# Sixteen weighted rows: one running sum, or four scalings in place and one reduction

## The reference, cut to what matters

```
scores, idx = top_k(sim, 16)              # per half key, 128 candidates
score = scores[0][..., :, None] + scores[1][..., None, :]
final_scores, pk_idx = top_k(score, 16)   # the 16 best pairs
kv_scores = softmax(final_scores)
k = einsum('bnhk,bnhkd->bnhd', kv_scores, keys_table[ind])
v = einsum('bnhk,bnhkd->bnhd', kv_scores, values_table[ind])
sim = einsum('bihd,bjhd->bhij', q, k)     # causal softmax, attention, projection
```

## Time and profile before

| what | value |
|---|---|
| profiled execution | 2909.09 us, span 2907.2 us |
| median of the runs | 2908.06 us |
| DVE busy | 2381.6 us, 82% of the span |
| POOL busy | 1961.6 us, 67% |
| PE busy | 1606.5 us, 55% |
| ACT busy | 762.2 us, 26% |
| DMA | mean 100 GB/s |

### The profile page before, as it was taken

One profiled execution on the slowest core, in us unless ns is written; L12 is line 12 of the kernel. 1 busy time (PEld: TensorE's weight loads), 2 busy tenths in 40 slices (PEclk: granted clock), 3 DMA queues, 4 the chain that ended last, 5 costly groups with the idle time before them and its releaser, 6 DMA issues. The chain is left out here.

```text
span 2907.2 us, 31873 instructions
## 1 busy us (share of the span) xinstructions
PE 1606.5 (55%) x7386; PEld 1234.3 (42%) x7386; DVE 2381.6 (82%) x8326; ACT 762.2 (26%) x1884; POOL 1961.6 (67%) x2064
## 2 busy tenths in 40 slices
PE   6847735565456445563555445554555445654555
PEld 6846624453334334442344334442344333432444
DVE  6678889999788888888888878888888878888873
ACT  5737611222122211221122112221122112221122
POOL 0001767777777777777777777777777777777774
PEclk8958856786578656785677656775678567765677
DMA  4200223333333333333333333333333333333332
GB/s 159 96 1 10 79 86 106 108 105 106 105 108 106 107 105 105 108 105 106 105 108 105 106 105 108 105 106 106 105 108 105 106 105 108 105 107 105 105 105 76
DMA packets 109528, 291.26 MB, mean 100 GB/s; under 512 B 34128, under 2 KB 41808, under 8 KB 107344
## 3 DMA queue, kind: packets, MB, share of 16 engines
q0 software_dynamic: 98304, 268.57, 32.6%
q1 hardware_dynamic: 10080, 20.97, 2.1%
q10 hardware_dynamic: 1008, 0.33, 0.0%
HBM read 288.69 MB, written 1.05 MB: 100 GB/s over the span
## 5 line engine op out<-in xcount | busy, mean ns | idle before, releaser
L282 POOL DMA_INDIRECT ring<-table,rows x2048 | 1954.1, 954 | 749.7 <-issue 587.3
L736 DVE SCALAR_TENSOR_TENSOR ps<-ring,wgt,ps 128x256 f32<-128x256 f32 x1792 | 865.5, 483 | 316.6 <-DMA ring<-table,rows 290.3
L1529 PE MATMUL ps<-ident,work 128*128 128x128 f32 x1088 | 261.3, 400 | 531.2 <-PEq L1522 531.2
L1529 PEld LDWEIGHTS ps<-ident,work 128*128 128x128 f32 x1088 | 202.0, 211 | 586.1 <-issue 586.1
L1543 PE MATMUL ps<-pts,work 128*128 128x128 f32 x2176 | 422.2, 360 | 35.4 <-PEq L1541 34.6
L1543 PEld LDWEIGHTS ps<-pts,work 128*128 128x128 f32 x2176 | 384.7, 267 | 84.1 <-issue 81.6
L1514 PE MATMUL ps<-work,qT 128*128 128x512 f32 (+3 forms) x576 | 312.3, 683 | 65.3 <-PEq L1511 65.3
L1249 ACT ACTIVATE pts<-ps 128x512 f32<-128x512 f32 (+2 forms) x320 | 168.8, 533 | 337.9 <-ACTq L1248 337.6
L1241 ACT ACTIVATE work<-ps,nmax 128x128 f32<-128x128 f32 (+15 forms) x128 | 149.4, 1167 | 327.5 <-ACTq L1239 327.5
L1506 PE MATMUL ps<-ident,work 128*128 128x128 f32 x128 | 46.8, 366 | 322.8 <-PEq L1504 322.7
L1514 PEld LDWEIGHTS ps<-work,qT 128*128 128x128 f32 x576 | 125.5, 239 | 196.9 <-issue 196.9
(11 more groups left out here) (234 smaller groups left out, 2688.5 us busy)
## 6 DMA issues: line engine op xcount, KB each, us to landing
ring<-table,rows POOLq DMA_INDIRECT x2048, 2.8
staged<-adj_in SPq DMA_DIRECT2D x16, 1024.0 KB, 4.9
xs<-x_in SPq DMA_DIRECT2D x4, 256.0 KB, 6.4
wpkq<-w_pkq SPq DMA_DIRECT2D x8, 128.0 KB, 2.6
out<-xs SPq DMA_DIRECT2D x1, 832.0 KB, 4.4
keyd<-pk_keys SPq DMA_DIRECT2D x16, 32.0 KB, 2.8
wo<-w_o SPq DMA_DIRECT2D x8, 64.0 KB
out<-xs SPq DMA_DIRECT2D x1, 192.0 KB, 2.1
```

Of the source, the lines that this page charges most:

```text
L282: nc.gpsimd.indirect_dma_start(ring[:, t % RING, k, :], None, table_d, bass.IndirectOffsetOnAxis(ap=rows[:, t % RING, k:k + 1], axis=0),). ...
L736: return v.scalar_tensor_tensor(out, row, w, acc_ps, ALU.mult, ALU.add)
L1529: ins = m.transpose(ps[:, 2 + (parity + b) % 2, j % 4 * P:(j % 4 + 1) * P], prob[:, t % 2, j * P:(j + 1) * P], ident[:, :])
```

## The change

The sixteen dependent multiply-adds go. In their place, `scale_rows(t, q)` multiplies the four rows of quarter q in the ring by their weights, in place, in one instruction of 4 x 256 elements whose second operand is the weights, each repeated 256 times. When all four quarters are scaled, `add_rows(t)` sums the sixteen rows with one `tensor_reduce` of 4096 elements to 256: it reads, for each of the 256 columns, the sixteen values that lie 256 elements (1 KB) apart. The weights `wgt` move from SBUF to 64 columns of PSUM bank 0, where the running sum no longer lives; `acc` in SBUF becomes `first_kv`. Where the multiply-adds with their `settle()` stood between two pieces of the search, a `settle()` or a `v.drain()` takes their place. Semaphores between engines are as they were: a slot is still freed, and `kv_full` still raised, when the whole sum of the tile is done.

```diff
-        wgt = sb("wgt", [P, 4, TOPK])
-        acc = sb("acc", [P, 2, 2 * D])
+        first_kv = sb("first_kv", [P, 2 * D])
-        acc_ps = ps[:, 0, 0:2 * D]
+        wgt = ps[:, 0, 3 * D + 64:3 * D + 64 + 4 * TOPK].rearrange("p (s k) -> p s k", s=4)
...
-            def sum_rows(t, k):
-                row, w = ring[:, t % RING, k, :], wgt[:, t % 4, k:k + 1]
-                if k == 0:
-                    return v.tensor_scalar(acc_ps, row, w, None, ALU.mult)
-                out = acc_ps if k < TOPK - 1 else kv[:, t, :] if t > 0 else acc[:, 0, :]
-                return v.scalar_tensor_tensor(out, row, w, acc_ps, ALU.mult, ALU.add)
+            def scale_rows(t, q):
+                some = ring[:, t % RING, q * QK:(q + 1) * QK, :]
+                w = wgt[:, t % 4, q * QK:(q + 1) * QK].unsqueeze(2).to_broadcast([P, QK, 2 * D])
+                v.tensor_tensor(some, some, w, ALU.mult).then_inc(dve_done, c.one())
+            def add_rows(t):
+                out = kv[:, t, :] if t > 0 else first_kv[:, :]
+                return v.tensor_reduce(out, ring[:, t % RING, :, :].rearrange("p k c -> p c k"), X, ALU.add)
...
                 landed(h, t, 0)
-                sum_even(t, 0)
+                scale_rows(t, 0)
                 if find:
                     find_replace(a)
                 if out:
                     add_out_1((t - 2) % T)
...
-                sum_odd(t, 1)
-                sum_even(t, 2)
+                landed(h, t, 1)
+                scale_rows(t, 1)
+                settle()
                 if out:
                     add_out_2((t - 2) % T)
                 if find:
                     find_second(a)
                 if prev and (t - 1) % T < 8:
                     score_max((t - 1) % T)
-                sum_odd(t, 3)
-                landed(h, t, 1)
-                sum_even(t, 4)
+                v.drain()
                 if find:
                     find_index(a)
                 if prev and (t - 1) % T >= 8 and not (last and t == T - 1):
                     score_max((t - 1) % T)
-                sum_odd(t, 5)
-                sum_even(t, 6)
+                if weigh:
+                    weigh_1((t + AHEAD - 1) % T)
+                landed(h, t, 2)
+                scale_rows(t, 2)
+                settle()
                 if find:
                     find_rows(a)
                 if weigh:
-                    weigh_1((t + AHEAD - 1) % T)
-                sum_odd(t, 7)
-                landed(h, t, 2)
-                sum_even(t, 8)
+                    weigh_2((t + AHEAD - 1) % T)
+                v.drain()
                 if find:
                     find_pairs(a)
-                if weigh:
-                    weigh_2((t + AHEAD - 1) % T)
-                sum_odd(t, 9)
-                sum_even(t, 10)
+                landed(h, t, 3)
+                scale_rows(t, 3)
+                settle()
                 if find:
                     find_best(a)
-                sum_odd(t, 11)
-                landed(h, t, 3)
-                sum_even(t, 12)
-                if find:
+                    v.drain()
                     find_best_replace(a)
-                sum_odd(t, 13)
-                sum_even(t, 14)
-                if find:
+                    v.drain()
                     find_best_second(a)
-                settle()
                 if t == 0:
-                    sum_rows(t, TOPK - 1).then_inc(dve_done, c.one())
+                    add_rows(t).then_inc(dve_done, c.one())
                     settle()
                 else:
-                    sum_rows(t, TOPK - 1).then_inc(kv_full, 1)
+                    add_rows(t).then_inc(kv_full, 1)
                     v.drain()
```

More of the change, by code:

```diff
@@ L759, in landed @@
                 dve.wait_ge(gathered[t % RING][q], h * (16 * QK * (T // RING)) + 16 * QK * (t // RING + 1))
-            def sum_even(t, k):
-                sum_rows(t, k).then_inc(dve_done, c.one())
-            def sum_odd(t, k):
-                settle()
-                sum_rows(t, k).then_inc(dve_done, c.one())
-                settle()
             def find_halves(t):
@@ L808, in step @@
                 if t == 1:
-                    v.tensor_copy(kv[:, 0, :], acc[:, 0, :]).then_inc(kv_full, 1)
-                sum_odd(t, 1)
-                sum_even(t, 2)
+                    v.tensor_copy(kv[:, 0, :], first_kv[:, :]).then_inc(kv_full, 1)
+                landed(h, t, 1)
+                scale_rows(t, 1)
+                settle()
                 if out:
```

## The result

The changed kernel takes 3299.22 us (median of 4 runs, 3296.64 to 3301.6) against 2906.16 us for the kernel before (four runs now, 2904.01 to 2908.72), a ratio of 1.1353 with a 95% interval of 1.1336 to 1.1371. I had forecast slower, but 2968 us with a range to 3010. The direction was right, the size was not: +393 us in place of +60.

The account below looks back on a forecast made before the run. POOL's gather issue was taken as the limit; DVE's step, 17.28 - 7.35 + 4.9 + 4.54 + 0.68 = 20.05 us, uses the whole slack, so DVE's chain from step 0 gives 2968 us, own range 2935 to 3000, widened to 2922 to 3010.

Parts of the forecast that it names:

- The limit before, and the slack: Kernel before: POOL's gather issue sets the period, 20.01 us a tile; DVE needs 17.28 us, leaving 2.73 us a step.
- the scalings: DVE's new multiplications of ring quarters by their weights: 1.22 us each, four a step, 4.9 us.
- The sums that go: DVE's removed first multiply, seven pairs of multiply-adds (6.34 us), and last one with its drain: 7.35 us a step.
- the drains: Four pauses a step between dependent search pieces on DVE, 0.17 us each: 0.68 us, bounds 0 to 1.0.
- the late start: DVE begins step 0 at 378.74 us and, its pace now equal to POOL's, never makes up that lateness.
- the loop's returns: The loop over heads goes back five times; DVE's waits there, formerly in the slack, add 17.5 us.
- the last four steps: End of kernel, no search: 11.7 us to step 124's `kv`, then 14.8, 15.0 and 18.6 to the next ones.
- the hand-over through PE: From `kv` to score maximum: 6.51 us for tile 14; rival: a wait every step, 3095 us, chance 0.03.
- The reduction: DVE's new 4096-element sum each step: 4.40 us without stride penalty, 4.54 us with its drain.
- the strided reduction is slower: Rival: two cycles an element in DVE's reduction, 4.3 us more a step, about 3515 us; chance 0.08.
- The rule that I had cited beside the rival: Trainium skill, on SBUF reads by DVE's reduction: lines of 16 bytes, each access to a new line pays a penalty.
- POOL as the limit: Rival: step under about 19.6 us, DVE catches up, gathers decide; 3.6 us more, 2912 us, chance 0.07.

Follow-up runs that it names:

- the second ladder: Kernel before plus 22 DVE instructions behind its end (reductions, products, copies, dense or strided); 16-element reductions took 0.16 us dense, 0.18 us strided.

## Why the prediction was right or wrong

**The limit before, and the slack: right.** Two spare reductions cost nothing, three cost 79 us, and without the scalings the time goes back to 2915. POOL's pace is the floor in both.

**The sums that go, the scalings, the drains: right, as a sum.** The scaling measured 1.21 us (1.22 forecast). With a dense reduction of 4.40 us (4.40 forecast) the step is 20.07 us (20.05) and the time 2969.19 (2968). The sums that go and the drains were not measured one by one; they are shown only in this total. (Seven pairs of 0.91 us are 6.37 and not the 6.34 of my sum, which is nothing here.) The terms of the sum that have no rows of their own, the late start, the loop's returns and the last four steps, are in that number too. That it lands within 1 us is partly luck: step 124 begins at 2877.31 us (2878.4 forecast), and from there to the end it takes 91.4 us (88.4), 1.3 us of it in the hand-over through PE for tile 14, 7.8 us where I had 6.5. The two misses have opposite signs. Alone, the late start and the returns together are shown by the spare reductions, within 9 us.

**The reduction: the step that failed.** I wrote "I take no penalty; the upper end is a full second cycle on every element, 4.3 us more". It measured 7.05 us, 2.65 us more than the 4.40 of the sum. 128 steps of it are 339 us, and 2968 + 339 = 3307, against 3299.22 measured. The mechanism was my own rival, "the strided reduction is slower", to which I gave 0.08; its price was a bound, the whole of the dense time once more (4.3 us), where 0.6 of it is the fact, so its 3515 us was too high as well.

Why did I discard it? By one row, 172 ns against 174 ns for 16 elements. At the true rate 16 elements cost 16 x 0.63 = 10 ns more, some 20 in the one pair of the second ladder. The two rows are single instructions, and they didn't begin alike: the dense one (L389) stood behind a wait, the strided one (L607) began while the instruction before it still ran. The dense ones of that size that begin in this way, reciprocals aside, took 110, 111, 167, 167, 167 and 172 ns. So the row could not show the effect: its scatter was wider than what I asked of it, and I multiplied its silence by 256. The rule that I had cited beside the rival was definite, and this row was too weak to outweigh it.

**The range.** It ended at 3010, while a rival of 3515 stood beside it. The only evidence against that rival was a row that could not see it, and no row of fitting size told the two ends of the cost apart. So the range should have reached it.

**The other rivals.** POOL as the limit did not come, and the hand-over through PE did not become a wait: DVE waited 2.8 us for scores between 700 and 2800 us, all told.

## What to carry to other kernels

Count two things when instructions are merged: the fixed parts that go, and the elements that pass through the engine once more. Here 11 fixed parts were saved and 4096 elements a step were added, and the slack of 2.7 us was gone even with a dense order. Read and write SBUF with neighbouring elements next to each other; a reduction across rows in SBUF cost 1.6 times its dense form here. And before a small row is used as evidence of no effect, work out how large the effect would be in that row, and compare it with the scatter of its neighbours.

## What the runs showed of the hardware that I had not expected

- On DVE, float32 in SBUF 16 bytes or more apart takes 1.6 times the dense time (7.0 us for 4096 elements, dense 4.42), in a reduction as in a product, read or written; with both inputs strided 8.63 us. 8 bytes apart is free, 12 bytes is between (5.53). A strided copy takes 4.61 us, a dense one 2.29. In PSUM 512 bytes apart is free for a reduction (2.29 and 2.29 us for 2048 elements).
- A gather issue of POOL that begins beside a dense addition of 2048 elements with both inputs in SBUF stands until the addition is over and ends 0.82 us after it (126 of 126); POOL becomes 171 us busier over the run.
- For one set of runs the kernels took 33% to 51% longer, with engines standing on "issue" between instructions of unchanged duration; 12 minutes later, on the chip of the same number, this was gone. In such a state even ratios to the kernel before mislead, so look at that kernel's time before using any other.
